# A linear attention loop in three overlapped stages, with products in 32-row tiles and numerators with 64 stationary columns

## The reference

```
q, k, v = split(x @ w_qkv.T);  q, k = rope(q), rope(k)
q_phi = elu(q) + 1;  k_phi = elu(k) + 1
kv_prefix = cumsum(k_phi[..., :, None] * v[..., None, :], axis=time)
k_prefix  = cumsum(k_phi, axis=time)
num   = einsum('bthd,bthdm->bthm', q_phi, kv_prefix)
denom = sum(q_phi * k_prefix, -1)
attn  = (num / (denom + 1e-6)) @ w_o.T
gate  = sigmoid((x[t] - x[t-1]) @ w_gate.T + b_gate)
x = x + gate * attn
```

## Time and profile before

| | |
|---|---|
| Median of 3 runs | 6257.24 us (6253.01 to 6261.46) |
| The profiled execution's own time | 6261.02 us |
| Its span in the profile | 6259.3 us |
| PE busy | 5185.6 us (83%) |
| PEld busy | 4217.9 us (67%) |
| DVE busy | 4407.7 us (70%) |
| ACT busy | 3747.8 us (60%) |
| POOL busy | 2032.6 us (32%) |

### The profile page before, as it was taken

How to read it: one execution, slowest core, us unless ns; L and a number is a source line. 1 busy time by engine, 2 the same in 40 slices (tenths; PEclk the granted TensorE clock), 3 DMA queues, 4 the chain that set the end, 5 groups by cost and what they waited for, 6 DMA issues and landing times. The chain is left out here.

```text
span 6259.3 us, 141962 instructions
## 1 busy us (share of the span) xinstructions
PE 5185.6 (83%) x41656; PEld 4217.9 (67%) x41656; DVE 4407.7 (70%) x11808; ACT 3747.8 (60%) x12063; POOL 2032.6 (32%) x1699
## 2 busy tenths in 40 slices
PE   5996959992499977999779997799968999699994
PEld 3665858982377766777667776677757777577773
DVE  4554666777477776777867777677777777677777
ACT  1112423341488855888568884688837888388882
POOL 0000000002244433444344442444424444244441
PEclk7876979996799999999999998999989999799997
DMA  0000200000011010000110001100010000100001
GB/s 18 0 0 14 59 9 1 0 0 31 23 23 23 22 41 23 22 22 22 42 24 22 22 22 42 24 22 22 22 44 22 22 22 22 44 22 22 22 22 48
DMA packets 103558, 144.77 MB, mean 23 GB/s; under 512 B 65414, under 2 KB 72859, under 8 KB 103131
## 3 DMA queue, kind: packets, MB, share of 16 engines
q1 hardware_dynamic: 94155, 109.63, 7.8%
q0 software_dynamic: 9232, 33.12, 1.6%
HBM read 49.13 MB, written 2.10 MB: 8 GB/s over the span
## 5 line engine op out<-in xcount | busy, mean ns | idle before, releaser
L1463 POOL TENSOR_TENSOR d_qk<-d_qk,d_sin_terms 128x512 f32<-128x512 f32 x792 | 995.1, 1277 | 1505.5 <-DVE d_sin_terms L1899 1505.5
L1782 ACT ACTIVATE d_probs<-d_S_ps,d_neg_max 128x96 f32<-128x96 f32 x3096 | 1016.2, 351 | 239.7 <-DVE d_neg_max L1928 239.7
L1899 DVE TENSOR_TENSOR d_qk<-d_A_ps,d_tables 128x512 f32<-128x512 f32 x816 | 564.4, 692 | 582.0 <-ACT d_squares L1745 581.9
L1469 POOL TENSOR_TENSOR d_qk<-d_qk,d_inv_norm 128x1024 f32<-128x1024 f32 x396 | 744.8, 1901 | 511.7 <-DVE d_inv_norm L1922 511.7
L1576 PEld LDWEIGHTS d_S_ps<-d_kT,d_q_blocks 128*128 128x128 f32 x6240 | 802.0, 192 | 4.1
L1576 PE MATMUL d_S_ps<-d_kT,d_q_blocks 128*128 128x96 f32 x6240 | 801.4, 271 | 0.0
L1782 ACT ACTIVATION_READ_ACCUMULATOR d_probs<-d_S_ps,d_neg_max 128x1 f32 x3096 | 671.7, 217 | 0.0
L1533 PE MATMUL d_A_ps<-d_wqkv_hi,d_xT_hi 128*128 128x512 f32 x1212 | 599.8, 495 | 18.1 <-DVE d_sin_terms L1899 13.4
L1540 PE MATMUL d_T_ps<-d_ident,d_qk 128*128 128x128 f32 x3168 | 504.2, 282 | 128.4 <-POOL d_qk L1469 105.7
L1899 DVE TENSOR_TENSOR d_sin_terms<-d_A_ps,d_tables 128x512 f32<-128x512 f32 x816 | 555.5, 681 | 0.0
L1586 PE MATMUL d_PT_ps<-d_ident,d_probs 128*96 128x128 f32 (+1 forms) x3072 | 473.9, 277 | 93.2 <-DVE d_probs L1937 93.2
(11 more groups left out here) (391 smaller groups left out, 10430.6 us busy)
## 6 DMA issues: line engine op xcount, KB each, us to landing
d_v_early<-d_v SPq DMA_DIRECT2D x198, 256.0 KB, 3.0
d_v_early<-d_v SPq DMA_DIRECT2D x198, 128.0 KB, 2.3
d_tables<-L_ffn_rotary POOLq DMA_DIRECT2D x7, 2048.0 KB, 9.7
d_qk<-L_ffn_Wqkv POOLq DMA_DIRECT2D x21, 512.0 KB, 4.2
d_xs<-d_xb SPq DMA_DIRECT2D x96, 63.5 KB
d_xs<-d_xb SPq DMA_DIRECT2D x48, 127.0 KB
ax_fp_blocks<-L_ffn_blocks_gu SPq DMA_DIRECT2D x16, 256.0 KB, 3.9
ax_fp_scales<-L_ffn_scales_gu SPq DMA_DIRECT2D x64, 64.0 KB, 3.5
```

Source lines behind the costliest of these rows:

```text
L1463: nc.gpsimd.tensor_tensor(c4[:, :, s, :], c4[:, :, s, :], s4[:, :, 1 - s, :], ALU.add).then_inc(rotated, 1)
L1469: nc.gpsimd.tensor_tensor(r3, r3, rn[:, b, k, :].unsqueeze(2).broadcast_to([P, HEADS, HD]), ALU.mult).then_inc(scaled, 1)
L1782: nc.scalar.activation(pr[:, g, n, seen_columns(g)], S[g % 2][:, n * SEEN:(n + 1) * SEEN], ACT.Exp, bias=nmax[:, g, n:n + 1], accum_out=de ...
L1899: nc.vector.tensor_tensor(terms[:, k, cols].rearrange("p (h d) -> p h d", d=HD), A[(c + 1) % 2][:].rearrange("p (h d) -> p h d", d=HD), ta ...
```

## The change

The same results are computed for the same 32 tiles. What differs:

- **Products.** `kx` and its zeroing go. k is copied whole into `kT` by one ACT copy, and the product of group g takes `kT[32g : 32g + 32]` as its stationary operand (32 rows by 128 columns) and the same 32 rows of `qx`, 512 columns.
- **Masked queries.** `qx` is written by ACT in four copies with the column of `head4` as the scale, no longer by DVE in one instruction.
- **Numerators.** Each head takes two matmuls, one for each half of 64 columns of the masked product, into the two halves of the partitions of `num_b`: 32 per tile, no longer 16.
- **Order.** The lists of the engines are written as `step(u)`, in which work of tiles u - 1, u and u + 1 alternates. On PE: three groups of numerators of u - 1, its attention transpose and output projection, the projections of u + 1, and between them the transposes, update, products, state and first numerators of u. On DVE the division, gate and sum of tile u - 1 and the rotation of u + 1 stand between the masks of u.
- **Buffers.** The attention transpose goes into the bank `o_b`, the state's update has one buffer for each batch, and a semaphore `state_read` keeps the state from being written before it has been read.

The diff, cut to its core (common indentation removed):

```diff
-kx = m2.sb("k_groups", [P, B, 4, P])
+kT = m2.sb("kT", [P, B, P])
-upd = m2.sb("state_update", [P, W])
+upd = m2.sb("state_update", [P, B, W])
...
-    nc.gpsimd.memset(kx[:], 0.0).then_inc(zeroed, 1)
     nc.gpsimd.memset(va[:], 1.0).then_inc(zeroed, 1)
...
+    def transpose_phi(u, b, first=False):
         pe.wait_ge(phi_ready, u + 1)
+        if not first:
+            pe.wait_ge(qx_ready, u * 4)
+            pe.wait_ge(kT_ready, u)
+            pe.wait_ge(qT_ready, u)
         for k in range(2):
...
-        if more:
-            project(u + 1, 1 - b)
-        pe.wait_ge(qx_ready, u + 1)
-        pe.wait_ge(kx_ready, u * 4 + 4)
-        for g in range(4):
-            pe.wait_ge(masked, u * 4 + (g + 1))
-            nc.tensor.matmul(s_b[g % 2][:], kx[:, b, g, :], qx[:, b].rearrange("p h t -> p (h t)"),
-                             start=True, stop=True).then_inc(s_ps, 1)
+    def products(u, b, g):
+        pe.wait_ge(qx_ready, u * 4 + 4)
+        pe.wait_ge(kT_ready, u + 1)
+        pe.wait_ge(masked, u * 4 + (g + 1))
+        rows = slice(32 * g, 32 * g + 32)
+        nc.tensor.matmul(s_b[g % 2][:], kT[rows, b, :], qx[rows, b].rearrange("p h t -> p (h t)"),
+                         start=True, stop=True).then_inc(s_ps, 1)
...
-        nc.tensor.matmul(num_b[:, 0:W], qT[:, b, :], state[:, b, :], start=True, stop=True)
+        nc.tensor.matmul(num_b[:, 0:W], qT[:, b, :], state[:, b, :], start=True, stop=True).then_inc(state_read, 1)
...
-        for g in range(4):
-            pe.wait_ge(masked, u * 4 + (g + 3))
-            for h in range(4 * g, 4 * g + 4):
-                last = nc.tensor.matmul(num_b[:, h * VW:(h + 1) * VW], pr[:, g, h % 4, :],
+    def numerators(u, b, g):
+        pe.wait_ge(masked, u * 4 + (g + 3))
+        for h in range(4 * g, 4 * g + 4):
+            for half in range(2):
+                rows = slice(64 * half, 64 * half + 64)
+                last = nc.tensor.matmul(num_b[rows, h * VW:(h + 1) * VW], pr[:, g, h % 4, rows],
                                         va[:, b, h * VW:(h + 1) * VW], start=False, stop=True,
                                         skip_group_check=True)
-        last.then_inc(num_ps, 1)
+        if g == 3:
+            last.then_inc(num_ps, 1)
+    def transpose_attn(u):
         pe.wait_ge(at_ready, u + 2)
-        nc.tensor.transpose(T_b[:, 0:P], at[:], ident[:]).then_inc(aT_ps, 1)
+        pe.wait_ge(gated, u + 2)
+        nc.tensor.transpose(o_b[:, P:2 * P], at[:], ident[:]).then_inc(aT_ps, 1)
+    def project_out(u):
         pe.wait_ge(aT_ready, u + 1)
-        pe.wait_ge(gated, u + 2)
...
+    def step(u, b, first=False, last=False):
+        if not first:
+            numerators(u - 1, 1 - b, 1)
+        if not last:
+            project_qk(u + 1, 1 - b)
+        transpose_phi(u, b, first)
+        if not first:
+            numerators(u - 1, 1 - b, 2)
+            numerators(u - 1, 1 - b, 3)
+        update(u, b)
+        products(u, b, 0)
+        if not last:
+            project_v(u + 1, 1 - b)
+        products(u, b, 1)
+        if not last:
+            project_gate(u + 1, 1 - b)
+        if not first:
+            transpose_attn(u - 1)
+        products(u, b, 2)
+        if not first:
+            project_out(u - 1)
+        from_state(u, b)
+        numerators(u, b, 0)
+        products(u, b, 3)
...
+    def copy_q_heads(u, b):
+        act.wait_ge(qkT_ps, u + 1)
+        for h in range(4):
+            nc.scalar.activation(qx[:, b, h, :], T_b[:, 0:P], ACT.Identity, scale=head4[:, h:h + 1]
+                                 ).then_inc(qx_ready, 1)
+    def copy_k(u, b):
+        act.wait_ge(qkT_ps, u + 1)
+        nc.scalar.activation(kT[:, b, :], T_b[:, P:2 * P], ACT.Copy).then_inc(kT_ready, 1)
...
-        for g in range(4):
-            nc.scalar.activation(kx[32 * g:32 * g + 32, b, g, :], T_b[32 * g:32 * g + 32, P:2 * P], ACT.Copy
-                                 ).then_inc(kx_ready, 1)
-        if more:
-            from_projection(u + 1, 1 - b)
...
+        nc.scalar.activation(aT[:], o_b[:, P:2 * P], ACT.Copy).then_inc(aT_ready, 1)
+    def step(u, b, first=False, last=False):
+        gate_tanh(u, b)
+        copy_q_heads(u, b)
+        copy_k(u, b)
+        if not first:
+            copy_attn(u - 1)
+        if not last:
+            copy_v(u + 1, 1 - b)
+        copy_q(u, b)
+        if not last:
+            exps(u + 1, 1 - b)
...
-    phis(0, 0, 0)
-    phis_end(0, 0)
-    def tile(j, b, more=True):
-        u = j * 2 + b
-        v.wait_ge(qkT_ps, u + 1)
-        v.wait_ge(kx_ready, u * 4 + 4)
-        nc.vector.tensor_tensor(qx[:, b], T_b[:, 0:P].unsqueeze(1).broadcast_to([P, 4, P]),
-                                head4[:].unsqueeze(2).broadcast_to([P, 4, P]), ALU.mult).then_inc(qx_ready, 1)
-        if more:
-            phis(u + 1, j + b, 1 - b)
-        for g in range(4):
-            v.wait_ge(s_ps, u * 4 + (g + 1))
-            nc.vector.tensor_tensor(pr[:, g], s_b[g % 2][:].rearrange("p (h t) -> p h t", h=4),
-                                    causal[:].unsqueeze(1).broadcast_to([P, 4, P]), ALU.mult).then_inc(masked, 1)
...
+        v.wait_ge(state_ready, u + 1)
+        nc.vector.tensor_tensor(upd[:, b, :], upd_b[:, 0:W], blocks[:], ALU.mult).then_inc(upd_masked, 1)
...
-        nc.vector.tensor_tensor(state[:, b, :], state[:, b, :], upd[:], ALU.add).then_inc(state_ready, 1)
+        v.wait_ge(state_read, u + 1)
+        nc.vector.tensor_tensor(state[:, b, :], state[:, b, :], upd[:, b, :], ALU.add).then_inc(state_ready, 1)
...
-        if more:
-            phis_end(u + 1, 1 - b)
+    def gate(u, b):
...
+    def step(u, j1, b, first=False, last=False):
+        if not last:
+            cosines(u + 1, j1, 1 - b)
+        if not first:
+            denominators(u - 1)
+        if not last:
+            sines(u + 1, j1, 1 - b, 0)
+        if not first:
+            inverses(u - 1)
+        if not last:
+            sines(u + 1, j1, 1 - b, 1)
+        if not first:
+            attention(u - 1)
+        mask_products(u, 0)
+        if not last:
+            rotated_sum(u + 1, 1 - b)
+        mask_products(u, 1)
+        if not last:
+            negatives(u + 1, 1 - b)
+        mask_products(u, 2)
+        if not first:
+            gate(u - 1, 1 - b)
+        if not last:
+            phis(u + 1, 1 - b)
+        if not first:
+            add_update(u - 1, 1 - b)
+        mask_update(u, b)
+        mask_products(u, 3)
+        if not first:
+            add_gated(u - 1)
...
```

More of the change, by code:

```diff
@@ new lines, in _ @@
+                    project_qk(0, 0)
+                    project_v(0, 0)
+                    project_gate(0, 0)
+                    step(0, 0, first=True)
+                    with pe.Fori(0, STEPS // 2 - 1) as i:
+                        for par in range(2):
+                            step(i * 2 + (1 + par), 1 - par)
+                    step(STEPS - 1, 1, last=True)
+                    for g in range(1, 4):
+                        numerators(STEPS - 1, 1, g)
+                    transpose_attn(STEPS - 1)
@@ L758, in _ @@
+                    project_out(STEPS - 1)
                 @block.scalar
@@ L784, in tile, with copy_attn @@
-                        act.wait_ge(aT_ps, u + 1)
[L785 to L791, removed]
+                    def copy_attn(u):
+                        act.wait_ge(aT_ps, u + 1)
+                        nc.scalar.activation(aT[:], o_b[:, P:2 * P], ACT.Copy).then_inc(aT_ready, 1)
@@ L793, in _ @@
+                    exps(0, 0)
+                    step(0, 0, first=True)
+                    with act.Fori(0, STEPS // 2 - 1) as i:
+                        for par in range(2):
+                            step(i * 2 + (1 + par), 1 - par)
+                    step(STEPS - 1, 1, last=True)
+                    copy_attn(STEPS - 1)
                 @block.vector
@@ L800, in _, with cosines, sines, rotated_sum @@
                     nc.vector.nop().then_inc(state_ready, 2)
[L801 to L803 removed]
+                    v.wait_ge(zeroed, 2)
+                    def cosines(u, j, b):
                         v.wait_ge(qkv_ps, u + 3)
                         src = qk_b[:, 0:2 * D].rearrange("p (h d) -> p h d", d=AD)
[L807 removed]
                         nc.vector.tensor_tensor(rc[:, b, :].rearrange("p (h d) -> p h d", d=AD), src,
[L809 removed]
+                                                rope[:, 0, bass.ds(j, 1), :].broadcast_to([P, 2 * AH, AD]), ALU.mult
+                                                ).then_inc(cos_done, 1)
+                    def sines(u, j, b, s):
                         src4 = qk_b[:, 0:2 * D].rearrange("p (h d two) -> p h d two", d=AD // 2, two=2)
                         dst4 = rs[:, b, :].rearrange("p (h d two) -> p h d two", d=AD // 2, two=2)
[L812 to L815 removed]
+                        tab = rope[:, 1, bass.ds(j, 1), :].rearrange("p j (d two) -> p j d two", two=2)[:, :, :, s]
```

(34 more changed lines are left out.)

49 lines of the change are left out of this document (25 added, 24 removed).

## The result

| | Before | After |
|---|---|---|
| Median, runs taken side by side | 6255.12 us (6250.91 to 6261.46, 4 runs) | 6376.04 us (6373.89 to 6379.16, 4 runs) |
| Profiled execution's span | 6259.3 us | 6374.2 us |
| Period of a tile in the loop | 13.86 us | 17.77 us |
| Granted clock, 310 to 520 us | 0.79 | 0.50 |
| PE busy in that window | 190 of 210 us | 210 of 210 us |

The ratio is 1.0193 (95% interval 1.0175 to 1.021). The forecast was 6140 us, the range 6095 to 6225: the time lies outside it, on the other side. Rival 1, the clock that doesn't hold, had named 18.4 us a tile and 6403 us, with a chance of 0.12.

The account below looks back on a forecast made before the run. PE was taken as the bound; products 3.44, other matmuls 2.41, numerators 1.98, switches 1.8, second loads 0.4 and waits 0.2 gave 10.2 us per tile against 13.86, 117 us saved over 32 tiles: 6140 us, range 6095 to 6225.

Parts of the forecast that it names:

- Rival 1: Loop's clock stays at 1.2 GHz and stream terms double: 18.4 us a tile, 146 us slower, 6403 us; chance 0.12.
- The clock: PE in the loop: full clock throughout, since no numerator stretch exceeds about 1.1 us, where before it was 3.6 to 4.5.
- Period: Time per tile in the loop: 10.2 us, where the kernel before takes 13.86 us.
- second loads of the 32-row products: Within each 32-row product the second load may not hide behind the first matmul: 0.1 us each, 0.4 us a tile.
- Numerators: 64 records of 64 columns in alternating output halves, 0.031 us apart: 1.98 us a tile.
- Changes of shape: PE switching between whole-array matmuls, 32-row products and 64-column numerators: 12 a step at 0.15 us, 1.8 us.
- ACT: Four masked queries and k copied in 2.85 us, just before product 0 at 3.0; the tightest place in the step.
- the walk's 0.15 us of slack: Step traced from first numerators: ACT's masked queries and k ready at 2.85 us, product 0 starting at 3.0.
- DVE, masks and tail: DVE at 6.4 us per tile delivers masks before PE wants them; the serial tail is covered by the next tile's work.
- Fewer contraction rows save nothing here: Four products on PE keep 512 columns, so eight records at 0.43 us stay at full price, 3.44 us.

Follow-up runs that it names:

- e13_filler3: Kernel after the change with three discarded whole-array matmuls of 512 columns added ahead of each 32-row product; 6480.3 us.
- e1_full_rows: Kernel after the change, but products contract all 128 rows of zero-padded kx, with k copied by ACT in four pieces; 6141.6 us, ratio to before 0.9817.
- e5_dve_queries: e1_full_rows with masked queries made by DVE in one instruction from ACT's SBUF copy of q; 6107.8 us, ratio to before 0.9757.
- e10_merged: e5_dve_queries with product 3 moved ahead of the first numerators, two changes of shape less per step; 6090.0 us, ratio to before 0.9728.
- e9_paired: Kernel after the change with its 32-row products next to each other in pairs, 0 with 1 and 2 with 3; 6240.3 us.
- e2_rows64: As e1_full_rows, but products contract the 64-row half of kx and qx that holds their 32 rows; 6381.4 us.
- e12_filler: Kernel after the change with one discarded whole-array matmul of 512 columns added ahead of each 32-row product; 6609.4 us.

## Why the prediction was wrong

The step that failed is **The clock**: "I therefore take full clock throughout". It argued from the length of low-column stretches alone, and took columns streamed as the thing that counts, whatever the number of rows. The runs show that rows count: the same order with the same columns has 0.96 with 128 rows and 0.50 with 64 or 32. I had listed this as rival 1 and priced it nearly right (18.4 us a tile for 17.8, +146 us for +121), but gave it 0.12. That no 32-row product was in the trace stood there on the rival's side, and only L1600 against it. The gap was a reason for a wide range and a larger chance: a mechanism whose sign decides the result, and of which the trace has no example, leaves both outcomes open. That the windowed transformer keeps its clock with L1600 said nothing on it, since L1600 narrows columns, not rows.

The other steps, read where the clock is high; these sizes were right:

- Period: 10.2 forecast. The list of the kernel after runs at 2.4 GHz in e13_filler3, where 26 of 31 steps take 20.71 us. Twelve discarded matmuls of 0.86 us are 10.3 of it, and there is one change of shape more: 10.2 to 10.4 us are left. That e1_full_rows, with 10.3 us and 6141.6 us, nearly meets the forecast of 10.2 and 6140 is luck, as it isn't the same sum. It has six changes of shape and the second loads of the 32-row products less (1.3 us by the forecast's prices), a wait of 0.94 us for k in four pieces, and 0.4 us from stretches at 1.2 GHz; its steps at 2.4 GHz take 9.89 us.
- Numerators: 0.031 us each forecast, 0.029 measured. At 1.2 GHz 0.057.
- Changes of shape: 0.15 each forecast, 0.14 measured between e5_dve_queries and e10_merged. The interval of one product alone shows only part of it: in e1_full_rows the product between two numerator groups takes 1.06 us (304.68 to 305.74) for 0.86, but the 16 numerators behind it take 0.57 (305.74 to 306.31), where 16 x 0.029 is 0.46. In e13_filler3 a 32-row product takes 1.06 too. The forecast's 0.1 for its second load was not measured by itself; the sum of e13_filler3 leaves room for it and for little more.
- ACT: with the one k copy PE doesn't wait for the masked queries. At 1.2 GHz and in e13_filler3, where the steps are long, this was no test of the walk's 0.15 us of slack. With four pieces of k they come late, by 0.94 us; with one copy at 2.4 GHz and no added work no run was made.
- DVE, masks and tail: no wait on them in PE, in e1_full_rows and e5_dve_queries too, right.
- "Fewer contraction rows save nothing here", with products at full price: right, 1.06 us alone at 2.4 GHz with 32 rows (e13_filler3) as with 128 (e1_full_rows), and the saving is there only side by side (e9_paired).

## What to carry to other kernels

Before a matmul is cut to fewer rows, look at the clock, not at PE's busy time: here a zero-padded operand with 128 rows was worth 234 us over one with 32. Where a low clock is the price of a shape, one run with the full shape tells it from waits, and discarded whole-array work tells whether the shape holds the clock down or only counts for little, if enough is added: one matmul for each product was too little here, three were enough. Leave small matmuls whole, or at least put their tiles next to each other (in pairs they were still 99 us behind the whole ones here), and don't scatter shapes through an ordered list: a single one-row matmul cost 0.35 us at each turn.

## What the runs showed of the hardware that I had not expected

- 64 contraction rows left the clock where 32 did, at 0.50, in a loop where 128 gave 0.96, although 96 of the 128 rows of the stationary operand held zeros (e2_rows64, e1_full_rows).
- PE was busy 210 of 210 us at 1.2 GHz: an engine without a gap is no sign that the clock is up.
- A change of tile shape cost 0.14 us at 2.4 GHz (e5_dve_queries, e10_merged), more than the interval of the one matmul in between shows.
- More work can be faster: e13_filler3 has eight discarded matmuls a step more than e12_filler and takes 129 us less.
- Two adjacent 32-row products in different rows run in the time of one (2.01 us for four records), with the clock still low (e9_paired). What makes the chip rate matmuls so, by rows or by shape of tile, these runs leave open: no product of between 65 and 127 rows was tried.
